# Layers 1 to 3 of a four-layer network without a setup block: the first input loaded ahead of the weights

## The reference, cut to what matters

```python
x = x + L0(_gn(x), ...)   # retention with a decay mask
x = x + L1(_gn(x), ...)   # mLSTM: up-projection, convolution, gates, causal weights, down-projection
x = x + L2(_gn(x), ...)   # 7x7 neighbourhood attention with a bias table
x = x + L3(_gn(x), ...)   # 7x7 windowed attention with a learned soft mask

def _gn(v, G=32, eps=1e-5):
    g = v.reshape(B_, H_, W_, G, C_ // G)
    m = jnp.mean(g, axis=(1, 2, 4), keepdims=True)
    s = jnp.var(g, axis=(1, 2, 4), keepdims=True)
    return ((g - m) / jnp.sqrt(s + eps)).reshape(v.shape)
```

## Time and profile before

| | us |
|---|---|
| median of 3 runs | 3466.73 (3464.69 to 3476.52) |
| the profiled execution's own time | 3469.34 |
| its span, first to last instruction | 3467.5 |
| mean granted TensorE clock | 0.953 of full speed |

### The profile page before, as it was taken

How to read it: one execution, slowest core, us unless ns; L and a number is a source line. 1 busy time by engine, 2 the same in 40 slices (tenths; PEclk the granted TensorE clock), 3 DMA queues, 4 the chain that set the end, 5 groups by cost and what they waited for, 6 DMA issues and landing times. The chain is left out here.

```text
span 3467.5 us, 94027 instructions
## 1 busy us (share of the span) xinstructions
PE 3105.6 (90%) x38656; PEld 1750.2 (50%) x38656; DVE 2211.7 (64%) x5202; ACT 2058.1 (59%) x4412; POOL 1155.1 (33%) x1446
## 2 busy tenths in 40 slices
PE   6999999999955999999999858999994899999996
PEld 2333333333312556566656526777772566666664
DVE  5878878887733667676777533545543566666765
ACT  2667676767633555545555515656562677777774
POOL 3433434343301222222222202222222455555554
PEclk9999999999976999999999979999997999999998
DMA  6777787777852333323323214445443233333332
GB/s 201 155 173 164 157 184 173 152 174 160 170 130 68 66 86 84 83 72 86 84 71 72 74 57 139 145 143 159 145 133 128 67 93 107 107 113 113 110 95 83
DMA packets 286233, 413.94 MB, mean 119 GB/s; under 512 B 25952, under 2 KB 242800, under 8 KB 264816
## 3 DMA queue, kind: packets, MB, share of 16 engines
q1 hardware_dynamic: 263248, 270.32, 26.0%
q0 software_dynamic: 18432, 134.23, 19.4%
q10 hardware_dynamic: 4128, 3.39, 0.3%
HBM read 219.30 MB, written 53.81 MB: 79 GB/s over the span
## 5 line engine op out<-in xcount | busy, mean ns | idle before, releaser
L732 DVE TENSOR_TENSOR l_probs<-l_psum,l_decay 128x1024 f32<-128x1024 f32 x512 | 598.6, 1219 | 163.5 <-PE l_psum L628 152.8
L780 ACT ACTIVATE l_sizes<-l_probs 128x2048 f32<-128x2048 f32 x256 | 487.6, 1910 | 300.3 <-DVE l_probs L732 293.0
L1793 ACT ACTIVATE l_logits<-l_logits,l_low 128x100 f32<-128x100 f32 x1024 | 374.7, 369 | 238.1 <-DVE l_low L1773 237.1
L1800 POOL TENSOR_TENSOR l_logits<-l_logits,l_inv 128x400 f32<-128x400 f32 x256 | 235.0, 918 | 737.7 <-DVE l_inv L1779 736.8
L628 PE MATMUL l_psum<-l_qk 32*128 32x512 f32 x2048 | 340.6, 646 | 7.9 <-POOL l_qk L866 4.2
L881 POOL DMA_DIRECT2D l_sizes<-l_sizes x128 | 111.5, 871 | 548.1 <-ACT l_sizes L780 536.1
L1632 POOL TENSOR_TENSOR l_E<-l_E,l_causal 128x1024 f32<-128x1024 f32 x64 | 153.3, 2396 | 378.0 <-DVE l_x_act L1365 224.8
L643 PE MATMUL l_psum<-l_probs,l_V 128*32 128x512 f32 x2048 | 270.6, 600 | 1.7 <-DVE l_probs L732 1.6
L299 PE MATMUL l_psum<-l_xT,l_w_up 128*128 128x512 f32 x512 | 232.2, 607 | 12.7 <-DVE l_row_var L1423 8.6
L1735 PE MATMUL l_psum<-l_keys,l_q_blocks 128*64 128x100 f32 x4096 | 230.6, 253 | 3.7 <-issue 2.4
L2726 POOL TENSOR_SCALAR l_soft<-l_dist,l_sharp,l_border 128x100 f32<-128x100 f32 x512 | 229.0, 464 | 0.1
(11 more groups left out here) (246 smaller groups left out, 6072.0 us busy)
## 6 DMA issues: line engine op xcount, KB each, us to landing
l_sizes<-l_sizes POOLq DMA_DIRECT2D x128, 1024.0 KB, 7.5
l_V_windows<-v_image SPq DMA_DIRECT2D x512, 100.0 KB
l_V_windows<-v_padded SPq DMA_DIRECT2D x512, 100.0 KB
l_E<-rows_c SPq DMA_DIRECT2D x64, 512.0 KB, 5.8
l_xT<-y SPq DMA_DIRECT2D x24, 1024.0 KB, 5.3
y<-l_res SPq DMA_DIRECT2D x32, 512.0 KB, 3.7
l_e_everywhere<-rows_e SPq DMA_DIRECT2D x112, 128.0 KB, 5.6
l_xT<-x SPq DMA_DIRECT2D x8, 1024.0 KB, 11.7
```

What stands on the lines that cost most here:

```text
L732: nc.vector.tensor_tensor(probs[:, N % 2, 2 * p:2 * p + 2, :], ring.region(name).rearrange("p (a n) -> p a n", a=2), decay[:, h:h + 2, s0: ...
L780: nc.scalar.activation(sizes[:, slot(N), :, :], probs[:, N % 2, :, :], ACT.Abs).then_inc(sized, 1)
L1793: nc.scalar.activation(e, e, ACT.Exp, scale=-1.0, bias=self.low[:, N % 4, i:i + 1], accum_out=self.total[:, N % 4, i:i + 1]).then_inc(self ...
L1800: nc.gpsimd.tensor_tensor(p, p, self.inv[:, N % 4, :].unsqueeze(2).to_broadcast([P, STEP, NKEY]), ALU.mult).then_inc(self.p_ready, 1)
```

## The change

In layers 1, 2 and 3 `load_all` and the setup block are gone, with their barriers. What they did stands at the head of the main block's lists. SP issues image 0 first, then the large weights; ACT issues the small ones before its first instruction. Two semaphores, `first_loaded` (the group matrix and the first projection's weights) and `rest_loaded` (all others), take the place of the one wait for all; each engine waits for a semaphore of its own where it first uses what another engine prepares.

```diff
 # layer 1
-        load_all(nc, L, [ ...
-        with nc.Block() as block:
...
-        L.barrier_and_clear()
 # SP
-                for b in range(3):
+                load(0)
+                sp.dma_start(wup[:, :, :], ktiles(A["L1_WupT"], HALVES)).then_inc(first_loaded, 16)
+                sp.dma_start(back[:, :, :, :].rearrange("p s i n -> p (s i n)"), A["L1_qkvT"]).then_inc(rest_loaded, 16)
+                sp.dma_start(gw[:, :, :, :].rearrange("p s i n -> p (s i n)"), A["L1_gate_w"]).then_inc(rest_loaded, 16)
+                sp.dma_start(wv[:, :, :].rearrange("p i n -> p (i n)"), A["L1_v"]).then_inc(rest_loaded, 16)
+                sp.dma_start(wdn[:, :, :], ktiles(A["L1_WdownT"], IT)).then_inc(rest_loaded, 16)
+                sp.dma_start(ident[:, :], A["ident"]).then_inc(rest_loaded, 16)
+                sp.wait_ge(folded, 1)
+                for b in (1, 2):
                     load(b)
 # PE
+                def fold():
+                    pe.wait_ge(rest_loaded, 272)
...
+                    m.then_inc(folded, 1)
+                pe.wait_ge(first_loaded, 32)
                 for u, t in layer1_steps():
+                    if u == -2 and t == 1:
+                        fold()
+                    if u == -1 and t == 0:
+                        pe.wait_ge(wq_ready, 1)
+                        pe.wait_ge(consts_ready, 1)
 # DVE: constants(), called after norm.collect of image 0
+                    dve.wait_ge(rest_loaded, 272)
...
+                    dve.wait_ge(folded, 1)
+                    nc.vector.tensor_copy(wg[:, :, 0:G], PS[:, 6 * BANK:6 * BANK + 2 * IT * G].rearrange(
+                        "p (i n) -> p i n", n=G)).then_inc(consts_ready, 1)
 # ACT: 13 DMA issues (group_mean, then 12 small constants) before its first instruction
 # layer 2
-                for b in range(3):
+                load(0)
+                sp.dma_start(wqkv[:, :, :], A["L2_WqkvT"].rearrange("(k p) n -> p k n", k=HALVES)).then_inc(first_loaded, 16)
+                sp.dma_start(wo[:, :, :], A["L2_WprojT"].rearrange("(k p) n -> p k n", k=HALVES)).then_inc(rest_loaded, 16)
+                sp.dma_start(bias[:, :, :].rearrange("p k n -> p (k n)"), A["L2_bias"]).then_inc(rest_loaded, 16)
+                sp.dma_start(window[:, :, :].rearrange("p k n -> p (k n)"), A["window"]).then_inc(rest_loaded, 16)
+                for b in (1, 2):
 # DVE, after norm.collect of image 0
+                dve.wait_ge(rest_loaded, 96)
+                nc.vector.tensor_scalar(qkv_b[:, 0:HALVES], qkv_b[:, 0:HALVES], HD ** -0.5, None, ALU.mult).then_inc(bias_ready, 1)
+                vstep(dve, nc.vector.tensor_tensor(bias[:, :, :], bias[:, :, :], window[:, :, :], ALU.add))
 # POOL, before norm.variance of image 0
+                nc.gpsimd.memset(w.q[:, :, :, :], 0.0).then_inc(q_cleared, 1)
 # layer 3, SP
+                load(0)
+                sp.dma_start(wqkv[:, :, :], in_halves(A["L3_WqkvT"])).then_inc(first_loaded, 16)
+                sp.dma_start(wo[:, :, :], in_halves(A["L3_WoutT"])).then_inc(rest_loaded, 16)
+                sp.wait_ge(keys_cleared, 1)
+                for s in range(2):
+                    zeros = keys[1][:, :, :].rearrange("p g n -> p (g n)")
+                    sp.dma_start(vimg[s].rearrange("n c -> (n c)").rearrange("(p n) -> p n", p=P), zeros).then_inc(cleared, 16)
+                for b in (1, 2):
                     load(b)
 # PE
+                pe.wait_ge(first_loaded, 48)
                 norm.average(nc, pe, ring, 0)
 # DVE
+                nc.vector.memset(keys[1][:, :, :], 0.0).then_inc(keys_cleared, 1)
...
+                nc.vector.memset(keys[0][:, :, :], 0.0)
                 norm.moments(nc, dve, vstep, 0)
                 norm.collect(nc, dve, ring, 0)
+                dve.wait_ge(rest_loaded, 144)
...
+                dve.wait_ge(cleared, 32)
 # POOL
+                pool.wait_ge(keys_cleared, 1)
+                nc.gpsimd.memset(w.q[:, :, :, :], 0.0).then_inc(q_cleared, 1)
```

More of the change, by code:

```diff
@@ L1032, in layer1 @@
-        with nc.Block() as block:
[L1033 to L1062, removed]
-                for r in range(2):
-                    nc.vector.memset(v1[:, :, :, :].rearrange("p s (i r) d -> p s i r d", r=2)[:, :, :, r, DH + r], 1.0)
-                heads = wv[:, :, :].rearrange("p i (r d) -> p i r d", r=2)
-                vstep(dve, nc.vector.tensor_reduce(wmean[:, :, :], heads, axis=AX.X, op=ALU.add))
-                vstep(dve, nc.vector.tensor_scalar(wmean[:, :, :], wmean[:, :, :], 1.0 / DH, 0.0, ALU.mult, ALU.add))
-                vstep(dve, nc.vector.tensor_tensor(heads, heads, wmean[:, :, :].unsqueeze(3).to_broadcast([P, IT, 2, DH]),
-                                                   ALU.subtract))
@@ L1460, in residual, with constants @@
                                             ring.region(name).rearrange("p (m n) -> p m n", m=HALVES), ALU.add).then_inc(ring.took(name), 1)
+                def constants():
+                    G = 2 * NH
+                    nc.vector.memset(eps[:, :], ROOT_EPS * 1e-6)
+                    nc.vector.memset(ones[:, :], 1.0)
+                    nc.vector.memset(ends[:, :, :], 0.0)
+                    nc.vector.memset(xm[0][:, :, 0:TAPS - 1], 0.0)
+                    nc.vector.memset(wg[:, :, :], 0.0)
+                    vstep(dve, nc.vector.memset(v1[:, :, :, :], 0.0))
+                    for r in range(2):
+                        nc.vector.memset(v1[:, :, :, :].rearrange("p s (i r) d -> p s i r d", r=2)[:, :, :, r, DH + r], 1.0)
+                    dve.wait_ge(rest_loaded, 272)
+                    heads = wv[:, :, :].rearrange("p i (r d) -> p i r d", r=2)
+                    vstep(dve, nc.vector.tensor_reduce(wmean[:, :, :], heads, axis=AX.X, op=ALU.add))
+                    vstep(dve, nc.vector.tensor_scalar(wmean[:, :, :], wmean[:, :, :], 1.0 / DH, 0.0, ALU.mult, ALU.add))
+                    nc.vector.tensor_tensor(heads, heads, wmean[:, :, :].unsqueeze(3).to_broadcast([P, IT, 2, DH]), ALU.subtract)
+                    dve.wait_ge(folded, 1)
+                    nc.vector.tensor_copy(wg[:, :, 0:G], PS[:, 6 * BANK:6 * BANK + 2 * IT * G].rearrange(
+                        "p (i n) -> p i n", n=G)).then_inc(consts_ready, 1)
+                    dve.wait_ge(consts_ready, 1)
                 conv_steps = 0
@@ L1472, in _ @@
                         norm.collect(nc, dve, ring, b)
+                        if u == -2:
+                            constants()
                     if t == 1 and 0 <= n < UNITS:
@@ L2292, in store, with in_halves @@
                     sp.dma_start(out[b, :, :, s], norm.x(b)[:, :, s]).then_inc(stored, 16)
-                for b in range(3):
+                def in_halves(w):
+                    return w.rearrange("(k p) n -> p k n", k=HALVES)
+                load(0)
[6 more added lines that the diff above has]
+                for b in (1, 2):
                     load(b)
@@ L2297, in _ @@
                     spread_args(0, half)
+                sp.wait_ge(cleared, 32)
                 for j in range(4):
@@ L2388, in _ @@
                             unit(unit_name(u, -1))
+                pe.wait_ge(rest_loaded, 144)
+                pe.wait_ge(consts_ready, 1)
+                pe.wait_ge(q_cleared, 1)
                 for j in range(8):
```

129 lines of the change are left out of this document (62 added, 67 removed).

## The result

| | before | after |
|---|---|---|
| median us | 3471.62 (3464.69 to 3476.61, 4 runs) | **3418.68** (3413.45 to 3422.22, 4 runs) |
| profiled execution, its span | 3469.34, 3467.5 | 3416.40, 3414.6 |
| mean granted clock | 0.953 | 0.962 |

The ratio is 0.9848, with a 95% interval of 0.9819 to 0.9877: 53 us faster, or 48 against the first three runs of before, from which the forecast was counted. Forecast were 3411.1 us and a gain of 55.6. The time is 7.6 us above that: inside the wide range of 3403 to 3423, a shade outside the narrow one of 3407 to 3418. Two steps of its sum don't hold, what the fold of layer 1 waits for and what the mask of layer 3 waits for, and the second costs 5 us.

A forecast was written before the change was run, and what follows sets the result against it. PE was taken to bound the bodies, and a serial chain of load, setup and normalisation the passages. Gains of 15.7 + 16.4 + 23.5 = 55.6 us from 3466.7 gave 3411.1 us, range 3407 to 3418, wide 3403 to 3423.

The forecast's parts named there:

- Layer 1: Layer 1's passage: the fold is late next, so the up-projection comes 15.7 us earlier, bounds 14.2 to 18.3.
- the volume of the heap: Layer 1's loads: image 0 ahead of the weights adds 2.6 us at 400 GB/s, so the fold begins at 1040.5.
- a warm start: Layer 1's up-projection directly behind the fold: a gain of 1.7 us, counted only in the rival of more than forecast (0.12).
- Layer 2: Layer 2's passage: image 0 is asked for 16.9 us earlier; gain 16.4 us, between 14.2 and 16.9.
- The addition's collision: Layer 2: DVE's bias addition falls on POOL's normalisation and costs 0 to 1.1 us, taken as 0.5.
- Layer 3: Layer 3's passage: image 0 is asked for 24.95 us earlier, DVE's clearing is late next; gain 23.5 us, bounds 20.5 to 24.9.
- The cover is 3 us: Layer 3: the zeros land at 2659.5, 3 us before DVE's first instruction that waits for them, at 2662.6.
- Bodies as long as now within 3 us each: Layers 1 to 3 behind their passages: a sign that each body's length stays within 3 us of before.
- The slow queues: Rival, all three passages: loads in one heap move at 250 GB/s; gain 50 us, 3417 us, chance 0.14.
- The heap's landing: Rival, all three passages: image 0 lands with the weights behind it; gain 42 us, 3425 us, chance 0.03.
- giving back in the bodies: Rival, bodies of layers 1 to 3: each loses 0.01 of clock, 24 us in all, 3435 us, chance 0.05.
- Slower: Rival, bodies of layers 1 to 3: clock falls below 0.94 and 64 us eat the gain; 3475 us, chance 0.02.

The follow-up runs named there:

- the repeat: The changed kernel unaltered, timed and traced once more: 3417.09 us (6 runs), ratio 0.9847 to the kernel before.
- The images' wait: Changed kernel, but in layer 3 SP waits for the small weights before asking for images 1 and 2: 3411.15 us, ratio 0.9850.
- the kernel with all edits: Changed kernel with fold behind first up-projections, bias addition between key copies, layer 3's zeros behind small weights, first key clearing behind statistics: 3413.52 us, ratio 0.9829.
- keys 0 late: Changed kernel, but in layer 3 DVE clears the first key tile behind the statistics, not before them: 3416.69 us, ratio 0.9869.

## Why the prediction was right, and where it was not

- **The mechanism** held. The body of each layer follows from its first product, and the passages shorten singly and together by the same amounts. Passages gave 16.6 + 16.2 + 18.7 = 51.5 us of the 52.9 between the two spans; layer 0 gave 1.0 and the bodies, in sum, 0.4. That the bodies cancel so well is luck of these two traces: in the repeat the passages gave 52.6 us, the bodies took 13.8 us more than before, and the span was 36.9 us shorter. In the medians too, a miss of a few us either way is within what the bodies do.
- **Layer 1** (forecast 15.7 at the up-projection): 38.54 - 21.95 = 16.6, inside its bounds. The fold began at +14.96 where I had +15.7. The term that bound was the one I had set aside: `l_gate_b` landed 8.4 us after its issue, as before, at 1038.8 or +15.0; I had taken the volume of the heap, +15.7. The fold ran at 0.50 once more. The up-projection directly behind it still began at 0.50 and ran at 1.00 from its fourth microsecond on, before from its fifth: 8.42 us against 8.76, 0.3 of the 1.7 that a warm start was worth. Over the seven traces with the fold directly in front it took 7.77 to 8.51, over the three of the old layer 1 8.60 to 8.76. The Trainium skill (TensorE: Matmul & The Clock Gate, Part 1) says that sustained PE work lifts the clock; here the 7.2 us of the fold passed at 0.50, and the clock rose in the third microsecond of the up-projection.
- **Layer 2** (16.4): 28.78 - 13.22 = 15.6 at the values, 16.2 at the scores, the point that counts. The statistics were not held by POOL's clearing. The addition's collision cost 0.73 on POOL where I took 0.5, and 0.86 at the values, as long as the two ran together; half of the overlap was too little, nearly all of it is what the trace shows.
- **Layer 3** (23.5): 38.90 - 15.27 = 23.6 at the projection, DVE's 1.2 us of delay included. The step that failed is "DVE's first instruction that now waits for `cleared` ... The cover is 3 us", and with it "waits for PE, not for the store of zeros". I checked only the zeros. They were in by +17.9 (2611.1 + 14.3, the longer of the two landings below), later than my +15.9, but a microsecond ahead of PE. But `rest_loaded` stands ahead of `cleared` in DVE's list, and I had priced ACT's queue by volume ("some small DMAs"). It came at +23.3, and the square at +23.90 where PE would have allowed about +19. The gain at the scores was 18.7: 4.8 us short. The images' wait shows the cause: the same small weights land 5.8 us sooner when the two images stay back. The view of L2280 in the changed kernel, for the zeros:

```profile
DMA to landing us min/median/max: 9.6/11.9/14.3
```

- **Bodies as long as now within 3 us each**: 981.5, 526.2 and 738.3 against 978.6, 531.4 and 736.4, so 2.9, 5.2 and 1.9. Layer 2's fails the bound, but that bound was too narrow for one kernel against itself: the same changed layer 2 took 537.6 in a repeat.
- **Rivals.** The slow queues, as one rate for the heap, did not appear: the fold came earlier than forecast. By the number alone that rival's 3417 us was nearer to the 3418.7 than the forecast, but for another reason: it took 21 us for layer 3 by a slow heap, and 18.7 came of a small weight's wait. The heap's landing is excluded by the statistics at +5.2. No giving back in the bodies is seen in the first trace. "Slower" was far off. Layer 3's 18.7 lies outside the bounds I had set for it, 20.5 to 24.9.

## What to carry to other kernels

When loads are taken out of a setup block and put beside the work, ask of every semaphore wait which of its members is issued last, on which queue, and what the other queue issues meanwhile; a 1 KB constant behind 7 MB of another queue can be the latest of all. Bring first what the first consumer waits for, and hold the prefetches that nobody needs yet until the last constant is in. Where a fold is done once, put it behind the first large products (6.0 us at the gates here), and see that no table load moves behind its wait. Moving a clearing behind the statistics is no such rule: it gave 0.6 us at one projection and cost 1.7 at another.

## What the hardware showed that I had not expected

- **Small DMAs beside a full queue.** Ten small DMAs on ACT's queue, 0.33 MB, took from 5.3 to 18.5 us each to land while SP's queue moved 7.15 MB, in 1264 packets to their 1344. Their bytes don't order them: 1 KB took 9.2 and 18.5 us, 64 KB 5.3 and 16.1. When they were issued and what SP's queue then held does. The equal counts speak for a price by the packet, but no run varied the number of packets of a small DMA.
- **Which pairs of DVE and POOL block each other.** POOL's clearing (6.92 us) left DVE's statistics at their 2.47 us and stopped a scaling of two columns. DVE's two-input addition of 1.09 us lengthened POOL's application by 0.73 in 0.86 us of overlap. DVE's clearing stretched POOL's first variance operation from 0.20 to 2.52 us in the kernel with all edits, where POOL began 0.25 us after the clearing had begun, and left it at 0.20 in the one with keys 0 late, where POOL began 0.12 us after that; why the one and not the other is open.
- **The scatter goes with the clock.** Ten executions of the changed kernel went from 3396.2 us at a mean granted clock of 0.967 to 3432.5 at 0.956. A least-squares line over 91 executions of the eleven kernels, with a level for each kernel, gives 29 us for 0.01 of clock and leaves 4.3 us. Between the two traces of the changed kernel PE's busy time, for the same instructions, rose from 3097.6 to 3116.3 us and the span from 3414.6 to 3430.6, so it is the products that take longer; what moves the clock no run shows. This is why edits of 5 us show in the passages of one trace, which repeat within 0.3 to 1.6 us, and not in a median of six runs. A clock of two kernels is not compared so, since the idle passages are counted in it.
